# Expert tiles of 256 rows in two blocks, and a router's steps moved in every engine's order

## The reference

```python
x = x + tanh(g_xattn[0]) * cross_attention_0(layernorm(x), ctx)   # 16 heads, 77 keys
x = x + tanh(g_ffn[0])   * real(ifft(fft(layernorm(x)) @ w)) + bias   # one 256x256 product
x = x + tanh(g_xattn[1]) * cross_attention_1(layernorm(x), ctx)   # with a bias by distance
x = x + tanh(g_ffn[1])   * moe(layernorm(x))

def moe(xf):                                  # 8 experts, 2 for each token
    scores = sigmoid(xf @ gate_w.T)
    _, sel = top_k(scores + expert_bias, 2)
    for e in range(8):
        w_t = sum(where(sel == e, top_scores, 0))
        h = square(relu((xf * w_t) @ w_up[e].T))          # 256 -> 512
        out += h @ w_down[e].T                            # 512 -> 256
```

## Time and profile before

| | |
|---|---|
| median of 3 runs | 2374.21 us (2369.73 to 2374.28) |
| profiled execution, its own time | 2374.52 us |
| its span, first to last instruction | 2372.7 us |
| busy: TensorE, VectorE, ScalarE, GpSimd | 83%, 56%, 32%, 40% of the span |
| mean granted clock of TensorE | 0.952 of full speed |
| DMA | 88.58 MB, 37 GB/s over the span |

### The profile page before, as it was taken

One profiled execution on the slowest core, in us unless ns is written; L12 is line 12 of the kernel. 1 busy time (PEld: TensorE's weight loads), 2 busy tenths in 40 slices (PEclk: granted clock), 3 DMA queues, 4 the chain that ended last, 5 costly groups with the idle time before them and its releaser, 6 DMA issues.

```text
span 2372.7 us, 44105 instructions
## 1 busy us (share of the span) xinstructions
PE 1969.1 (83%) x13970; PEld 1749.7 (74%) x14003; DVE 1319.2 (56%) x3668; ACT 748.8 (32%) x1509; POOL 957.8 (40%) x1332
## 2 busy tenths in 40 slices
PE   2798988989889898898988989888079888888884
PEld 1687877878778788788888878877067677677663
DVE  2466666666666666666666676665544333333331
ACT  2223323233232322323223233232244444444432
POOL 0344445344453444534444444442323333333333
PEclk7799999999999999999999999999589999999997
DMA  5000101000010100100001000010443333333332
GB/s 116 12 10 30 29 9 38 9 29 29 9 38 9 29 29 9 38 9 29 29 9 38 9 29 29 9 35 6 154 93 60 58 58 58 58 58 58 58 49 29
DMA packets 93909, 88.58 MB, mean 37 GB/s; under 512 B 26904, under 2 KB 87320, under 8 KB 93880
## 3 DMA queue, kind: packets, MB, share of 16 engines
q0 software_dynamic: 26160, 35.87, 8.8%
q1 hardware_dynamic: 67720, 52.33, 8.1%
HBM read 43.77 MB, written 44.39 MB: 37 GB/s over the span
## 4 chain that ended last, share of the span: by engine, by line
PE 47%; DMA 20%; issue 12%; DVE 8%; POOL 6%; ACT 5%; SPq 1%; POOLq 1%; DVEq 0%; ACTq 0%
PE scores L1088 25%; DMA out<-y,ids 19%; PE bank L1088 18%; POOL sorted_rows L667 3%; PE bank L1156 3%; DVE t_lo L893 1%; ACT routed L781 1%; DVE biased L970 1%; POOL rstd L614 1%; ACT t_hi L746 1%; DVE e L967 1%; ACT q_hi L751 1%; PE scores L1213 1%; POOL kb_hi L632 1%; ACT neg_mx L756 1%
## 5 line engine op out<-in xcount | busy, mean ns | idle before, releaser
L695 POOL DMA_INDIRECT out<-y,ids x136 | 211.8, 1557 | 461.3 <-ACT y L805 281.1
L614 POOL TENSOR_TENSOR rstd<-var,half_power 128x2 f32<-128x2 f32 x128 | 90.2, 705 | 568.6 <-DVE var L880 567.9
L1088 PE MATMUL scores<-vb,pr 128*128 128x136 f32 x2048 | 280.3, 279 | 0.7 <-ACT pr_rest L767 0.7
L1088 PEld LDWEIGHTS scores<-vb,pr 128*128 128x128 f32 x2048 | 256.9, 190 | 5.9 <-ACT pr_rest L767 4.1
L943 DVE TENSOR_REDUCE mx<-scores 128x8 f32<-128x512 f32 x256 | 169.6, 684 | 139.3 <-remote 81.5
L1072 DVE SCALAR_TENSOR_TENSOR h<-scores,relu 128x512 f32<-128x512 f32 x136 | 94.1, 692 | 272.6 <-ACT relu L799 266.7
L1088 PE MATMUL scores<-q_hi,kb_hi 128*128 128x256 f32 (+1 forms) x640 | 197.7, 309 | 34.5 <-ACT neg_mx L756 34.5
L746 ACT ACTIVATE t_hi<-bank 128x512 fp32r<-128x512 f32 x192 | 114.8, 598 | 346.3 <-PE bank L1156 346.1
L893 DVE TENSOR_TENSOR t_lo<-bank,t_hi 128x512 fp32r<-128x512 f32 x192 | 132.1, 688 | 120.8 <-ACT t_hi L746 117.9
L667 POOL DMA_INDIRECT sorted_rows<-routed,place x128 | 126.8, 990 | 169.2 <-ACT routed L781 138.1
L1088 PE MATMUL scores<-up_hi,xt_hi 128*128 x272 | 120.6, 443 | 84.5 <-DVE xt_lo L1066 84.3
(11 more groups left out here) (222 smaller groups left out, 5746.8 us busy)
## 6 DMA issues: line engine op xcount, KB each, us to landing
xe<-sorted_rows SPq DMA_DIRECT2D x136, 128.5 KB, 2.1
x<-x_rows SPq DMA_DIRECT2D x32, 256.0 KB, 2.9
out<-x_end SPq DMA_DIRECT2D x32, 256.0 KB, 3.0
raw<-w_up_t SPq DMA_DIRECT2D x8, 512.0 KB, 4.3
raw<-w_down_t SPq DMA_DIRECT2D x8, 512.0 KB, 4.6
ctx<-ctx_t SPq DMA_DIRECT2D x32, 77.0 KB, 2.7
out<-y,ids POOLq DMA_INDIRECT x136, 3.8
sorted_rows<-routed,place POOLq DMA_INDIRECT x128
```

The lines of the kernel that those rows point to most:

```text
L614: pool.tensor_tensor(rstd[u][:], var[u][:], half_power[:], ALU.pow).then_inc(sem(f"rstd_ready{u}"), 1)
L695: pool.indirect_dma_start(out=acc, out_offset=bass.IndirectOffsetOnAxis(ap=ids[j][:], axis=0), in_=y[j][:], in_offset=None, compute_op=ALU ...
L1088: last = pe.matmul(dst, w, m, start=n == 0, stop=n == len(pairs) - 1)
```

## The change

A tile has 256 rows in two blocks of 128: 72 tiles, 144 blocks. One load brings both blocks (`xe` is a ring of four tiles); everything from `x_turn` to `y` still goes by block. The adds of a tile's two blocks, which are of one expert and so of different tokens, don't wait for each other. `ids` and `y` are free again when the whole tile that last used them is in. Zero rows reach 256 rows behind each expert's last one, in two transfers for each. In part 1 `places` goes from slot 10 to slot 1 of the next half, `weights` from 10 to 9, `weigh` from 2 to 3, `send` from 3 to 5.

```diff
-NT = 2 * TOK // P + E
+NT = 2 * TOK // ROWS + E
+BLOCKS = NB * NT
 DEEP = 8
+RING = DEEP // NB
...
         def choose_steps(u, t):
-            return {9: [("columns", u, t)], 10: [("places", u, t), ("weights", u, t)]}
+            return {9: [("columns", u, t), ("weights", u, t)]}
 
         def send_steps(u, t):
-            return {2: [("weigh", u, t)], 3: [("send", u, t)]}
+            return {1: [("places", u, t)], 3: [("weigh", u, t)], 5: [("send", u, t)]}
...
-            for stage in ("weigh", "send"):
+            for stage in ("places", "weigh", "send"):
...
-            sp.wait_ge(sem("ended"), 16 * (E + 1))
+            sp.wait_ge(sem("ended"), 16 * NB * (E + 1))
...
-            def load(k, j):
-                if j >= DEEP:
-                    sp.wait_ge(sem("xe_used"), k * DEEP + (j - DEEP + 1))
-                    sp.wait_ge(sem("ids_ready"), k * DEEP + (j - DEEP + 1))
+            def load(k, i):
+                if i >= RING:
+                    sp.wait_ge(sem("xe_used"), k * DEEP + NB * (i - RING + 1))
+                    sp.wait_ge(sem("ids_ready"), k * DEEP + NB * (i - RING + 1))
                 carrier(sp)
-                row = sp.value_load(tile_table[0:1, bass.ds(k * DEEP + j, 1)], min_val=0, max_val=IDLE)
-                sp.dma_start(xe[j % DEEP][:], sorted_rows[bass.ds(row, P), :]).then_inc(sem(f"xe_in{j % DEEP}"), 16)
+                row = sp.value_load(tile_table[0:1, bass.ds(k * RING + i, 1)], min_val=0, max_val=IDLE)
+                sp.dma_start(xe[i % RING][:], sorted_rows[bass.ds(row, ROWS), :].rearrange("(b p) d -> p b d", p=P))\
+                  .then_inc(sem(f"xe_in{i % RING}"), 16)
...
-            for e in range(E + 1):
+            for e in range(NB * (E + 1)):
                 pool.indirect_dma_start(out=sorted_rows, out_offset=bass.IndirectOffsetOnAxis(ap=ends[:, e:e + 1], axis=0),
-                                        in_=zero_rows[:], in_offset=None).then_inc(sem("ended"), 16)
+                                        in_=zero_rows[:, e // (E + 1), :], in_offset=None).then_inc(sem("ended"), 16)
...
-                    pool.wait_ge(sem("added"), k * (DEEP * 16) + j * 16)
+                    if j % NB == 0:
+                        pool.wait_ge(sem("added"), k * (DEEP * 16) + j * 16)
...
             def down_part(k, j):
                 if j >= DEEP:
-                    act.wait_ge(sem("added"), k * (DEEP * 16) + (j + 1 - DEEP) * 16)
+                    act.wait_ge(sem("added"), k * (DEEP * 16) + ((j - DEEP) // NB + 1) * NB * 16)
...
             def xt_part(k, j):
                 if j >= DEEP:
-                    dve.wait_ge(sem("added"), k * (DEEP * 16) + (j + 1 - DEEP) * 16)
-                dve.tensor_copy(ids[j % DEEP][:], xe[j % DEEP][:, D:ROW]).then_inc(sem("ids_ready"), 1)
+                    dve.wait_ge(sem("added"), k * (DEEP * 16) + ((j - DEEP) // NB + 1) * NB * 16)
+                dve.tensor_copy(ids[j % DEEP][:], xe[j // NB % RING][:, j % NB, D:ROW]).then_inc(sem("ids_ready"), 1)
```

More of the change, by code:

```diff
@@ L199, in build @@
         own_row = sb1("own_row", [P, 1])
-        ends_f = sb1("ends_f", [P, E + 1])
-        ends = sb1("ends", [P, E + 1], U32)
+        ends_f = sb1("ends_f", [P, NB, E + 1])
+        ends = sb1("ends", [P, NB * (E + 1)], U32)
         count = sb1("count", [P, E])
@@ L254, in build @@
         raw = [sb2(f"raw{i}", [P, 1024]) for i in range(4)]
-        xe = [sb2(f"xe{i}", [P, ROW]) for i in range(DEEP)]
+        xe = [sb2(f"xe{i}", [P, NB, ROW]) for i in range(RING)]
         ids = [sb2(f"ids{i}", [P, 1], U32) for i in range(DEEP)]
@@ L444, in in_order @@
                 step(0, j)
-            with fori(0, NT // DEEP - 2) as k:
+            with fori(0, BLOCKS // DEEP - 2) as k:
                 for j in range(DEEP, 2 * DEEP):
                     step(k, j)
-            k = NT // DEEP - 2
+            k = BLOCKS // DEEP - 2
             for j in range(DEEP, 2 * DEEP):
@@ L542, in _ @@
                              a[name][n // 2].rearrange("(k p) n -> p k n", p=P)).then_inc(sem(f"raw_in{n % 4}"), 16)
[L544 to L548 removed]
+            def load(k, i):
+                if i >= RING:
+                    sp.wait_ge(sem("xe_used"), k * DEEP + NB * (i - RING + 1))
+                    sp.wait_ge(sem("ids_ready"), k * DEEP + NB * (i - RING + 1))
                 carrier(sp)
[L550 to L557 removed]
+                row = sp.value_load(tile_table[0:1, bass.ds(k * RING + i, 1)], min_val=0, max_val=IDLE)
+                sp.dma_start(xe[i % RING][:], sorted_rows[bass.ds(row, ROWS), :].rearrange("(b p) d -> p b d", p=P))\
+                  .then_inc(sem(f"xe_in{i % RING}"), 16)
+            for i in range(RING):
+                load(0, i)
+            with sp.Fori(0, NT // RING - 1) as k:
+                for i in range(RING):
+                    load(k, RING + i)
         @block.gpsimd
@@ L688, in _ @@
                 pool.wait_ge(sem(f"x_out{u}"), 16 * PAIRS)
-            with pool.Fori(0, NT // DEEP) as k:
+            with pool.Fori(0, BLOCKS // DEEP) as k:
                 for j in range(DEEP):
@@ L696, in _ @@
                                             in_=y[j][:], in_offset=None, compute_op=ALU.add).then_inc(sem("added"), 16)
-            pool.wait_ge(sem("added"), NT * 16)
+            pool.wait_ge(sem("added"), BLOCKS * 16)
         @block.scalar
@@ L1024, in _ @@
             after(dve.tensor_copy(tile_no[:], tile_table[:, 0:NT]))
-            after(dve.tensor_scalar(ends_f[:, 0:E], run[:], own_row[:, 0:1], None, ALU.add))
-            after(dve.tensor_scalar(ends_f[:, E:E + 1], own_row[:], float(IDLE), None, ALU.add))
-            dve.tensor_copy(ends[:], ends_f[:]).then_inc(sem("ends_ready"), 1)
+            for b in range(NB):
+                after(dve.tensor_scalar(ends_f[:, b, 0:E], run[:], own_row[:, 0:1], float(b * P), ALU.add, ALU.add))
+                after(dve.tensor_scalar(ends_f[:, b, E:E + 1], own_row[:], float(IDLE + b * P), None, ALU.add))
+            dve.tensor_copy(ends[:], ends_f[:].rearrange("p b e -> p (b e)")).then_inc(sem("ends_ready"), 1)
             after(dve.tensor_tensor(count[:], run[:], first_row[:], ALU.subtract))
-            after(dve.tensor_scalar(count_i[:], count[:], float(P - 1), None, ALU.add))
-            after(dve.tensor_scalar(tiles_i[:], count_i[:], P.bit_length() - 1, None, ALU.arith_shift_right))
+            after(dve.tensor_scalar(count_i[:], count[:], float(ROWS - 1), None, ALU.add))
+            after(dve.tensor_scalar(tiles_i[:], count_i[:], ROWS.bit_length() - 1, None, ALU.arith_shift_right))
             after(dve.tensor_copy(tiles_f[:], tiles_i[:]))
@@ L1034, in _ @@
                 after(dve.tensor_tensor(until[:, e:e + 1], until[:, e - 1:e], tiles_f[:, e:e + 1], ALU.add))
-            after(dve.scalar_tensor_tensor(out=shift[:, 1:E], in0=until[:, 0:E - 1], scalar=float(-P), in1=first_row[:, 1:E],
+            after(dve.scalar_tensor_tensor(out=shift[:, 1:E], in0=until[:, 0:E - 1], scalar=float(-ROWS), in1=first_row[:, 1:E],
                                            op0=ALU.mult, op1=ALU.add))
@@ L1275, in expert_of @@
             def expert_of(k, j):
-                return pe.value_load(tile_table[0:1, bass.ds(k * DEEP + (j + NT), 1)], min_val=0, max_val=E - 1)
+                return pe.value_load(tile_table[0:1, bass.ds(k * RING + (j // NB + NT), 1)], min_val=0, max_val=E - 1)
             def x_turn(k, j):
@@ L1340 @@
     aps = {k: nc.dram_tensor(k, v.shape, mybir.dt.from_np(v.dtype), kind="ExternalInput").ap() for k, v in arrays.items()}
-    out = nc.dram_tensor("out", [TOK + P, D], F32, kind="ExternalOutput").ap()
+    out = nc.dram_tensor("out", [TOK + ROWS, D], F32, kind="ExternalOutput").ap()
     build(nc, aps, out)
```

22 lines of the change are left out of this document (12 added, 10 removed).

## The result

The kernel after takes 2345.4 us (median of 4, 2343.2 to 2346.8), the one before 2374.2 beside it. The ratio is 0.9884, 95% interval 0.987 to 0.9898: faster by 1.2%, where 3.3% was forecast, and outside the forecast range of 2284 to 2310 and the wider one up to 2336. The profiled execution has a span of 2343.5. Since chips differ by some 0.3% (the kernel before took 2374, 2379 and 2381 on three of them), small differences are taken from the ratios to the kernel before on the same chip.

What follows compares the result with a forecast made beforehand. It took the experts' part to start bound by TensorE, then by GpSimd's adds waiting one for another. Experts -95, zero rows +11.4, loop +6 (count -24, transfers +30) made -78 from 2374.2: 2296, range 2284 to 2310, wider 2264 to 2336.

Steps and rivals of the forecast that it cites:

- Experts' part, -95: Adds of the experts' part: a tile's second add no longer waits, so TensorE sets 3.71 us a block; -95 us.
- dearer pair: Rival, experts' part: two adds in flight each land some 1.4 us later, 3.95 us a block, +34, 2330; chance 0.12.
- slower: Rival, experts' part: each add must finish before the next one's data, pace 4.61 again, 2428; chance 0.03.
- both in a row: Upper end for a tile's two adds without overlap: 8.7 us a tile, 4.3 a block.
- Zero rows, +11.4: Between the parts: 18 indirect transfers in place of nine, with nothing hiding them; +11.4 us.
- The count, -24: Loop over pairs: count moved behind `queries` shortens TensorE's wait and three clock falls in four vanish; -24 us.
- TensorE's wait at `queries`, forecast 1.3: Loop over pairs: of TensorE's 1.9 us wait some 0.6 goes and 1.3 stays, for `t_lo`.
- The transfers, +2.0 x 15 = +30: Loop, second half: moved transfers make the second norm's `rstd` 1.3 us late, plus 0.7 for a clock fall; +30 us.
- next to nothing: Loop, first half: cost of the same transfer move, as the norm behind has `values`' evacuation ahead of it.
- the transfers cost more: Rival, loop: each row transfer is held until one VectorE instruction ends, +41, loop +47, 2337; chance 0.11.

Runs made afterwards that it cites:

- slot 3 transfers: The kernel after with the row transfers back at slot 3 of both halves, the count staying at slot 1: 2256.0 us, ratio 0.9506.
- the spreads' wait: The kernel after, transfers still at slot 5, with GpSimd's second spread of the second layer waiting for VectorE's norm of the second block: 2272.7 us, ratio 0.9573.
- the 1.49 us case: A norm in the kernel after with the second half's transfers alone moved from slot 5 to slot 9: 2257.0 us, ratio 0.9489.
- the run on the stopped queue: The kernel after, transfers at slot 5, with GpSimd's second spread of the second layer waiting for GpSimd's own rstd: 2300.7 us, ratio 0.9671.

## Why the prediction was wrong

**Experts' part, -95: right.** First add to last was forecast 95 us shorter and is 92.9 shorter, at 3.71 us a block as taken. The rivals "dearer pair" and "slower" are out. One add at a time gives 4.58, above the 4.3 that I had worked out for both in a row, because each then has its own 0.86 behind its landing.

**Zero rows, +11.4: right** (10.7 from the first of them to the weights' load). Nothing hid them, as said. They cost their length because SyncE waits for them. Without the wait 10 of the 19 us go, and the other 9 are DMA's, which moves the weights and the zero rows at the same 310 GB/s.

**The count, -24: too small.** Measured 39 (slot 3 transfers) and 43 (slot 5). The mechanism was right, the size not: I took three falls in four to vanish, and all 22 did. By the intervals with and without one, 9 of them cost 1.2 us each and 13 cost 1.0: 24. The rest, with the transfers at slot 3, is in the intervals behind the first half (0.56 a pair less than the undisturbed ones of before), behind the second (0.35) and behind the fourth (0.2): 15 x 1.1 = 17. That makes 41 where 39 was measured. Why the second half's interval is shorter no run here shows. With the transfers at slot 5 I didn't break the 43 down. TensorE's wait at `queries`, forecast 1.3, is 1.30 and 1.03.

**The transfers, +2.0 x 15 = +30: this is the step that failed.** "It is 1.3 late, VectorE's `xn` and TensorE's turn at 1014.10 behind it" was right for `rstd` and wrong for what follows. The price is 89 us by the run that puts them back, 5.6 a pair in the second half and 0.57 in the first, where "next to nothing" was forecast. TensorE's wait is 5.62 where I had 3. I carried the norm's length of before (1.49, with TensorE's 1.00 behind it in the earlier trace rows) over as a constant, though its length comes from what GpSimd does beside it. Taking the spreads away gives 73 of the 89 back; stopping GpSimd's queue for an instant gives 45 to 51. The lateness alone, my mechanism, is within the 17 that are left with the spreads' wait, 8 of them the first half's. I also took one fall of 0.7 for a wait of 3 us; the 5.62 us wait brings a double stay, which costs about 1.3 us of the pair's period (against the run where the spreads wait, TensorE's wait is 3.69 longer and the interval 28.24 - 23.23 = 5.01).

The rival "the transfers cost more" came within 9 us of the result, but by luck, as its mechanism is another: the transfers take 966 ns in the median and 1220 at most, as in the earlier trace rows.

The Trainium skill's page "SBUF — State Buffer" (section "SBUF: two separate sides") names the two engines that got in each other's way here. It says that a pair of ports is an exclusive lock between a GpSimd instruction and a VectorE instruction in a two-port mode or with two SBUF inputs, held for the whole instruction by whichever starts first. Whether the norm, with one input of 128x256 in SBUF, runs in such a mode no trace here shows. I had used the page for descriptors alone, and there it still doesn't show. For the norm, the trace agrees that VectorE is shut out beside GpSimd's spread, for 0.7 us in the 1.49 us case (1.12 instead of 0.41). But one instruction is not the bound: in the 4.42 us case it is six in a row, 4.0 us. And starting first didn't help: in the run on the stopped queue the norm starts 0.05 us ahead of the spread, and its first instruction takes 1.23 all the same.

The sum by measured terms: -78 (tiles, zero rows) - 41 (count, the middle of 39 and 43) + 89 (transfers) = -30, measured -28.8.

What stays open: why the first instruction of the norm gets no turn between two spread instructions when GpSimd hasn't paused. A stop in GpSimd's queue just ahead of the spreads restores the turn, and that is shown; how its instructions are held ready no trace here shows.

## What to carry to other kernels

When a step is moved on GpSimd, look at what it pushes onto VectorE's instructions between SBUF buffers, not only at who waits for GpSimd: their length in the profile holds only for the order it was taken in. Here GpSimd, once it had no idle time left, took VectorE's turns away, and a wait that costs next to nothing gave them back. And try the parts of a change one by one: here two good ones (-78, -41) hid one bad one (+89) behind a gain of 1.2%.

## What the runs showed of the hardware

- VectorE's norm (two instructions, 128x256, SBUF to SBUF) takes 0.73 us alone, 1.49 beside GpSimd's three spreads when GpSimd was idle 2.8 us or more before the `rstd` ahead, 4.42 when it had no idle time there and no wait behind `rstd`, and 1.60 with a wait on its own semaphore in between. It is the first of the two instructions that is held each time. The `var` of 128x2, 0.17 us otherwise, took 1.68 at 1039.12. It started 0.6 us ahead of the first spread, beside the last row transfer, and ended with that spread's first instruction.
- The clock: 22 of 30 waits of TensorE for `hot_sum` (most 1.7 to 1.9 us) were followed by a stay at 1.2 GHz, none of the 29 waits of 1.0 to 1.3 at the same place after, and 14 of the loop's 15 waits of 5.6 us came with a double stay. TensorE's wait for `xn` came with one in 4 of 15 cases where it is 1.93 us long (the spreads' wait), in 14 of 15 where it is 2.79 (the stopped queue), and once where it is 1.06 (at 1632.85 in the kernel after). A stay takes 1.7 us of full clock but only 1.0 to 1.2 from the pair's period.
- Two adds that are in flight together for about 1 us don't slow each other enough to show: the next pair leaves 4.6 us after the second add, as the next add did one at a time (4.58 and 4.61), with DMA at 0.43.
